# Summing the middle tap of a depthwise convolution in TensorE's transposes for two of eight channel blocks

## What is computed

```python
y = einsum('bnh,boh->bno', x, W[id]) + bias[id]          # the input map of layer 1
h = bit_linear(y, w1)                                    # 256 -> 1024, rounded activations, ternary weights
h = depthwise_conv1d(h.transpose(0, 2, 1), conv_w, conv_b)   # three taps along the 512 tokens, one set per channel
h = silu(h.transpose(0, 2, 1))
x = x + bit_linear(h, w2)                                # 1024 -> 256
```

## Time and profile before

| what | value |
|---|---|
| median of 3 runs | 319.86 us |
| lowest, highest | 319.39 us, 322.47 us |
| span of the profiled execution, its only time on the page | 319.6 us |
| busy in that span | DVE 276.6, PE 264.5, POOL 259.2, ACT 240.6 us |

### The profile page before, as it was taken

One profiled execution on the slowest core, in us unless ns is written; L12 is line 12 of the kernel. 1 busy time (PEld: TensorE's weight loads), 2 busy tenths in 40 slices (PEclk: granted clock), 3 DMA queues, 4 the chain that ended last, 5 costly groups with the idle time before them and its releaser, 6 DMA issues. The chain is left out here.

```text
span 319.6 us, 6460 instructions
## 1 busy us (share of the span) xinstructions
PE 264.5 (83%) x1676; PEld 179.7 (56%) x1700; DVE 276.6 (87%) x606; ACT 240.6 (75%) x366; POOL 259.2 (81%) x402
## 2 busy tenths in 40 slices
PE   6679878869798887999889797989899898967574
PEld 6234334535455454566656665868587686745452
DVE  0778988896899989955899999999999999999671
ACT  4588897966776487567566888889989888978770
POOL 2567899996898988759999999998989799898310
PEclk9977799999999999999999999999999999999997
DMA  7995773579496368454430333445436373444764
GB/s 249 320 363 118 222 197 76 113 159 213 100 215 126 75 87 178 69 100 91 44 66 2 60 74 66 118 98 91 111 93 122 70 98 82 101 98 100 120 145 115
DMA packets 90745, 39.50 MB, mean 124 GB/s; under 512 B 73005, under 2 KB 88141, under 8 KB 90710
## 3 DMA queue, kind: packets, MB, share of 16 engines
q1 hardware_dynamic: 84532, 30.47, 46.8%
q10 hardware_dynamic: 6178, 8.62, 8.6%
HBM read 18.11 MB, written 4.19 MB: 70 GB/s over the span
## 5 line engine op out<-in xcount | busy, mean ns | idle before, releaser
L812 POOL TENSOR_TENSOR raw_all<-raw_all,mid 128x1024 f32<-128x1024 f32 x32 | 63.7, 2000 | 0.7 <-DVE raw_all L1025 0.7
L548 ACT ACTIVATE g<-banks,dqz 128x1024 f32<-128x1024 f32 x32 | 35.5, 1112 | 24.4 <-POOL r L757 21.2
L805 POOL TENSOR_SCALAR mid<-apad,taps,convb 128x512 f32<-128x512 f32 x64 | 48.8, 774 | 0.5 <-DVE apad L1018 0.5
L608 ACT ACTIVATE banks<-apad,taps 128x512 f32<-128x512 f32 x64 | 42.3, 682 | 6.9 <-DVE apad L1018 6.8
L970 DVE TENSOR_REDUCE am<-g 128x1 f32<-128x1024 f32 x32 | 38.6, 1211 | 8.6 <-ACT g L548 8.5
L1025 DVE SCALAR_TENSOR_TENSOR raw_all<-apad,taps,banks 128x512 f32<-128x512 f32 x64 | 45.8, 743 | 0.0
L1018 DVE TENSOR_TENSOR apad<-banks,dqb 128x512 f32<-128x512 f32 x64 | 40.9, 684 | 4.6 <-PE banks L1337 4.5
L757 POOL TENSOR_SCALAR r<-g,qs 128x1024 uint16<-128x1024 f32 x32 | 36.8, 1153 | 6.2 <-DVE qs L982 5.9
L1365 PE MATMUL banks<-tern,q1T 128*128 128x256 bf16 x256 | 33.8, 276 | 9.5 <-DMA q1T<-r 8.0
L1227 PE MATMUL banks<-tern,qT 128*128 128x512 bf16 x117 | 36.6, 388 | 5.5 <-ACT qcT L540 3.3
L627 ACT ACTIVATE r<-g,qs 128x1024 uint16<-128x1024 f32 x32 | 36.6, 1144 | 5.3 <-DVE qs L1044 3.2
(11 more groups left out here) (116 smaller groups left out, 561.5 us busy)
## 6 DMA issues: line engine op xcount, KB each, us to landing
out_y<-xs SPq DMA_DIRECT2D x32, 128.0 KB, 2.0
xs<-in_x ACTq DMA_DIRECT2D x7, 512.0 KB, 5.7
x2T<-in_xT ACTq DMA_DIRECT2D x4, 512.0 KB, 5.2
wl<-in_cwl SPq DMA_DIRECT2D x8, 256.0 KB, 2.7
xT<-in_xT ACTq DMA_DIRECT2D x3, 512.0 KB, 4.2
raw_all<-in_w1a ACTq DMA_DIRECT2D x1, 1024.0 KB, 5.0
cw<-in_cw SPq DMA_DIRECT2D x16, 64.0 KB, 5.0
gam<-in_gamma SPq DMA_DIRECT2D x8, 128.0 KB, 3.0
```

The lines of the kernel that those rows point to most:

```text
L608: act.activation(bank(BANK_U[g % 3]), apad[:, f, 2:S + 2], ACT.Copy, scale=taps[:, f, 2:3]).then_inc(p_last, 1)
L805: pool.tensor_scalar(mid[f // 2 % 2][:, f % 2, :], apad[:, f, 1:S + 1], taps[:, f, 1:2], convb[:, f:f + 1], ALU.mult, ALU.add).then_inc(p_ ...
L812: pool.tensor_tensor(c[:, 2 * q:2 * q + 2, :], c[:, 2 * q:2 * q + 2, :], mid[q % 2][:, :, :], ALU.add).then_inc(p_sum, 1)
```

## The change

In layer 1, tap_sum is no longer done for q = 3, blocks 6 and 7. Their middle taps go to a tile of their own, mid_last, with one buffer, and transpose_conv makes their transposed blocks in two steps: a transpose of conv that starts the PSUM block, and a transpose of mid_last that adds to it. So each transpose_conv has 10 instructions in place of 8. Waits change with it: the first transpose_conv of a batch waits for three sums, all eight first taps and all eight middle taps; middle_tap for blocks 6 and 7 of batch b waits until transpose_conv(b-1, 3), the last reader of mid_last, is done. The two buffers of mid now alternate over three sums per batch.

```diff
+        mid_last = sb("mid_last", [P, 2, S])
...
+        SUMS = TB - 1
...
-                wait(pool, p_sum, TB * b + f // 2 - 1)
-                pool.tensor_scalar(mid[f // 2 % 2][:, f % 2, :], apad[:, f, 1:S + 1], taps[:, f, 1:2],
+                q = f // 2
+                if q < SUMS:
+                    wait(pool, p_sum, SUMS * b + q - 1)
+                    out = mid[(SUMS * b + q) % 2][:, f % 2, :]
+                else:
+                    wait(pool, p_cT[TB - 1], b)
+                    out = mid_last[:, f % 2, :]
+                pool.tensor_scalar(out, apad[:, f, 1:S + 1], taps[:, f, 1:2],
                                    convb[:, f:f + 1], ALU.mult, ALU.add).then_inc(p_mid, 1)
...
-                                   mid[q % 2][:, :, :], ALU.add).then_inc(p_sum, 1)
+                                   mid[(SUMS * b + q) % 2][:, :, :], ALU.add).then_inc(p_sum, 1)
...
                 on(tap_sum, s - 1, 2)
-                on(tap_sum, s - 1, 3)
...
-                scale_of_down1(7, 3); middle_tap(1, 0); middle_tap(1, 1); tap_sum(0, 3); tap_sum(1, 0)
+                scale_of_down1(7, 3); middle_tap(1, 0); middle_tap(1, 1); tap_sum(1, 0)
...
-                middle_tap(1, 7); tap_sum(1, 2); tap_sum(1, 3)
+                middle_tap(1, 7); tap_sum(1, 2)
...
-                    pe.wait_ge(p_sum, TB * b + TB)
+                    pe.wait_ge(p_sum, SUMS * (b + 1))
+                    pe.wait_ge(p_first, KH * (b + 1))
+                    pe.wait_ge(p_mid, KH * (b + 1))
...
-                for f in range(KH):
-                    ins = pe.transpose(bank(BANK_C + f // KT)[:, (f % KT) * P:(f % KT + 1) * P],
-                                       conv[b % 2][:, f, k * P:(k + 1) * P], id32[:, :])
+                for f in range(2 * SUMS):
+                    pe.transpose(bank(BANK_C + f // KT)[:, (f % KT) * P:(f % KT + 1) * P],
+                                 conv[b % 2][:, f, k * P:(k + 1) * P], id32[:, :])
+                for f in range(2 * SUMS, KH):
+                    block = bank(BANK_C + f // KT)[:, (f % KT) * P:(f % KT + 1) * P]
+                    pe.matmul(block, conv[b % 2][:, f, k * P:(k + 1) * P], id32[:, :], start=True, stop=False,
+                              is_transpose=True)
+                    ins = pe.matmul(block, mid_last[:, f - 2 * SUMS, k * P:(k + 1) * P], id32[:, :], start=False,
+                                    stop=True, is_transpose=True)
```

## The result

| | kernel before | changed kernel |
|---|---|---|
| median (lowest to highest), 20 runs each | 321.35 us (317.95 to 323.25) | 322.61 us (320.17 to 324.95) |
| ratio to the kernel before | 1 | 1.006, 95% interval 1.0032 to 1.0087 |
| span of the profiled execution | 319.6 us | 322.2 us |

What follows compares the result with a forecast made beforehand. DVE was taken to pace layer 1 at about 18.4 us a batch, with a chain of DMA transposes and PE's down projections at the end. -0.6 (sy) + 0.4 (wait) + 0.7 (end) = +0.5 us: 319.86 becomes 320.3, range 317.6 to 324.2.

Steps and rivals of the forecast that it cites:

- What leaves POOL: Layer 1, POOL: eight additions of 1.98 us, one per batch, 15.8 us in all; none leaves DVE.
- What PE gains: transpose_conv on PE: two more transposes per call, 0.22 us a call at 0.11 each, upper bound 0.27 each.
- Rival C: PE: accumulating transposes run one after another at 0.27 us, 0.5 us in each of five windows, 322.8 at most; chance 0.05.
- The wait on POOL: POOL's middle taps 6 and 7 stall 2.7 us for the previous batch's last transpose_conv; charged +0.4 us over four slots.
- rival A: POOL's middle tap 6: the wait closes a binding loop, 0.79 us in each of four slots, +3.9, 323.8; chance 0.20.
- sy: DVE's instruction at L1006: no longer held up by POOL's addition in slot 3 of the fill, counted as -0.6 us.
- A's other sign: DVE waiting for L1301's result through ACT's evacuate, named as showing the forecast wrong in favour of rival A.
- DVE's idle time: Middle windows of layer 1: still under 0.3 us each, named as a sign that the forecast is right.
- The round trip: From a batch's first middle tap through call 3 to the next: 18.1 us against a slot of 18.4, so it closes.
- The end: After the last batch's sums: call (7,0) 1.3 us later, the end +0.4 to +1.2 us, taken as +0.7.
- The older DMA transpose: At the end: the transfer whose data PE needs at 303.28, taken as not touched by the change.
- rival B: Freer POOL helps: DVE's idle 0.80, sy's 0.72 and 1.0 at the end from a faster DMA transpose, 317.4; chance 0.15.

Runs made afterwards that it cites:

- pool_relief: Changed kernel with eight transposes per call and no wait at middle taps 6 and 7, leaving out those blocks' middle tap and bias; ratio to before 0.9983.
- extra_pe: Kernel before with blocks 6 and 7 transposed twice in each transpose_conv, POOL untouched; ratio to before 1.0010.
- warm_after: Changed kernel with six added matmuls into free bank 0 in PE's idle time before transpose_conv(0, 1); ratio to before 1.0022.
- four_sums_b0: Changed kernel with batch 0 done as before: its fourth sum on POOL, eight plain transposes per call; ratio to before 1.0052.
- two_buffers: Changed kernel with two buffers of mid_last, so middle_tap(b, 6) waits for transpose_conv(b-2, 3) only; ratio to before 1.0000.

## Why the prediction was right

It was right in direction and bound, and short in size: +0.5 us forecast, 1.9 (1.0 to 2.8) measured. Part of the agreement is luck, as the steps show:

- **What leaves POOL** (15.8 us): 16.3 by busy time. That this is worth nothing to the steady slots holds: pool_relief's took 73.57 us against 73.54.
- **What PE gains** (0.22 us per call): 1.25 us a call, the lower bound. Rival C is out. PE had room for it (extra_pe).
- **The wait on POOL** (2.7 us per slot): 3.0, above the 1.5 to 2.7 named as a sign. Its effect on DVE was put at +0.4 for four slots. The ten profiles with the added transposes of mid_last have +0.04 to +1.0, +0.4 in the mean, but nearly all of it comes with two slow DMA transposes that the prediction didn't think of: here the number is luck. What the wait itself does is what the prediction feared under rival A, at a small part of its price: sy at over 0.2 us in middle slots, 0.1 to 0.3 us in all where A had 3.2. A's other sign, DVE waiting for the evacuation of y, is there as well (0.18 us above), but from batch 3 on only in profiles with a slow transpose, and with two buffers too. DVE's idle time reached 0.33 us in one window, where under 0.3 was expected. The round trip closes, as worked out, and A as a loop that binds in every slot is out.
- **sy** in the fill (-0.6): -0.65, within 0.1 in all eleven profiles of kernels without POOL's fourth sums from batch 1 on (18.51 to 18.61 us against 19.12 to 19.22 with them).
- **The end** (call (7,0) 1.1 to 1.3 us later, round2(6, 3) 1.3, the end +0.4 to +1.2): the call came 1.15 us later, counted from batch 7's first dequant, round2(6, 3) 1.37, down2(6, 3) 0.36, the lower of the two times forecast for it, and round2(7, 3) 0.3 to 0.4 in the changed kernel's two profiles, 0.7 and 1.0 in those of warm_after and four_sums_b0. Up to there the chain was read right. The last final2 came 0.3 us sooner in one profile of the changed kernel and 1.5 later in the other; there it is the fall of the clock at the very end that decides. The older DMA transpose, of tile (6, 2), which the prediction took as untouched, took 3.0 us in place of 4.4, and the younger, of tile (6, 3), which rival B hoped for, 3.0 in place of 3.8. The first won nothing: PE then waited for DVE's final2(6, 1), "0.63 <-DVE xs L1056" above. The second made up 0.7 of round2(6, 3)'s 1.37.
- **What was missed:** the prediction priced nothing in the fill but sy's gain, and nothing for call (0,0) coming sooner. An earlier call (0,0) lengthened PE's idle time from 1.47 to 1.89 us, and in 2 of 4 profiles with 1.89 or 2.11 us the granted clock fell to half for some 3.5 us and cost 1.6. The rows of before that were read showed a full clock there. The Trainium skill, "TensorE: Matmul & The Clock Gate", section "Why this matters for your kernels", warns of idle gaps between bursts of matmuls. By that rule, the traces agree only in kind: the fall went when the gap was filled, but it came with gaps shorter than those the page names, and not in every execution.

How the 1.9 us divide stays open within about a microsecond. The four kernels with one buffer up to the end measured 1.006, 1.0059, 1.0052 and 1.0022; the four with a second buffer 1.0000, 1.0003, 0.9983 and 0.9999. Their means, 1.0048 and 0.9996, differ by 0.5%, 1.7 us, where the profiles show 1.0 to 1.7 up to round2(7, 3). Three of the second four also have the six matmuls in the fill, and only one of the first four, so the two repairs are not fully apart; but two_buffers, without the matmuls, measured 1.0000, and warm_after, with them and one buffer, 1.0022. So the larger part of the loss most likely hangs on the wait in the last batch, and the fall of the clock in the fill adds to it in some executions; how often was not measured. Without that wait the change wins 0.7 us at the end over the kernel before (29.9 against 30.61), and this and sy's gain pay for the steady slots.

## What to carry to other kernels

A wait that a pipeline hides in every steady slot can still cost once, where the pipeline drains (about 1.4 us here, of a wait of 3.5): look at the last round by itself, and give that round its own buffer. Relief for an engine that isn't the pace is worth, in the steady slots, at most the pace engine's idle time (0.80 us of windows here) and what the relieved engine holds up (0.6 us at sy), and both are known beforehand. A stretch that differs between profiles of one kernel is best sorted by the lengths of its DMA transfers before a theory is built on it. And when a wait goes in front of TensorE, ask what it waits for next: the same wait, moved on and made longer, can cost more than it did, through the clock (1.6 us in two profiles of four).

## What the runs showed of the hardware

Two fp32 transposes into one PSUM block, the second adding to the first, run at the plain transposes' spacing of 0.11 us. At one place, before transpose_conv(0, 1), the granted clock fell with an idle time of 1.89 us in two profiles and of 2.76 in one, did not with 1.89 and 2.11 in two others, and not once with 1.5 us or less, in nine. At the end, where idle times of about 1 to 2 us follow each other closely, it fell before PE's last matmul in ten of the fourteen profiles. A single DMA transpose of this kernel took 3.0 to 3.3 us from issue to landing or, at some tiles, up to 5.1, with no cause that the traces show; batch 1's last tile took 4.0 or more in every profile, others were slow only in some. A VectorE instruction of 0.17 us that starts while a GpSimd addition of 2.0 us is running ended with that addition, within 0.03 us, wherever it was lengthened in the middle slots.
